# Four expert half-steps, six transposes and the chain for the row maxima are moved and rewritten in an early-fusion transformer kernel

## The chip, the cores and the metric

The kernel runs on one core of a Trainium2 chip. The metric is the device time of one execution in microseconds. The engines are TensorE (PE, with its weight loads as PEld), VectorE (DVE), ScalarE (ACT), GpSimd (POOL) and SyncE (SP), which issues most DMAs. Each runs its own program in order, and they wait for each other through semaphores.

## What is computed

Sixteen images and sixteen texts go through one block. A tokenizer makes 49 image tokens of each image; with a class token and 128 text tokens they are 178 tokens of 192 channels. An attention layer, a second attention layer with standardised logits, and a top-2 mixture of four experts follow. Cut to what the change touches:

```python
# second attention (inside the ffn)
logits = jnp.einsum('bqhd,bkhd->bhqk', Q, K) * scale
logits = gamma * _zscore_last(logits, T)
probs = jax.nn.softmax(logits, axis=-1)
...
x = _layernorm(src + attn, ln1_g, ln1_b)
gate_scores = jax.nn.softmax(x @ Wg.T + bg, axis=-1)
top2_val, top2_idx = jax.lax.top_k(gate_scores, 2)
combine = (jax.nn.one_hot(top2_idx, E, dtype=x.dtype) * top2_val[..., None]).sum(axis=-2)
h = jax.nn.relu(jnp.einsum('btd,edf->ebtf', x, W1) + b1[:, None, None, :])
y = jnp.einsum('ebtf,efd->ebtd', h, W2) + b2[:, None, None, :]
ff = jnp.einsum('ebtd,bte->btd', y, combine)
return _layernorm(x + ff, ln2_g, ln2_b)
```

The first attention (s = 0 in the kernel) masks the diagonal of its logits; the second (s = 1) does not.

## The kernel before

**Rounds.** The 16 images are taken as eight pairs. After a first part (tokenizer, first attention of pair 0, weight preparation) come nine rounds. Round p works on three pairs at once: the second attention of pair b = p, the first attention of pair a = p + 1, and the expert network of pair m = p - 1; it also starts the front (transposes, query, key, value) of pair nxt = p + 2. Rounds 2 to 5 are all alike. Round 0 has no experts yet; round 6 has no nxt; round 7 has neither a nor nxt; the last has only experts.

**What sets the order.** The order is written out by hand: `pe_round`, `act_round` and `dve_round` each list the parts of a round. The expert network is cut into 50 half-steps. Step (u, even) makes the hidden tile u of 24: five products (L674) into bank 4 or 5, followed by a ReLU on ScalarE (L709). Step (u, odd) is the second layer of tile u - 1: three products (L696) into banks 6 and 7. The last two are the turn of the combine weights with the last second layer, and the bias product (L684). VectorE adds an expert's result (L724) at the first odd step behind the expert's last tile, that is at steps 13, 25, 37, and at step 48. How many half-steps run at which named point of a round is a table: `FILL` for rounds 1 to 5 and the last, `FILL_A7` for round 6, `FILL_B7` for round 7. All three engines go through the same points with the same numbers. Round 0 and the first part fill with idle products instead (`WARM`, L770).

**A round on TensorE**, in order: half-steps ("start"), transposes of the normalised tokens (L787), "norm", query product (L795), "query", key product (L795), "key", value product (L803), transposes of the keys (L916, L917), "kc", product of keys with themselves (L927), "g", product with the queries (L933), "u", sum over a head (L939), "ss"; then the first maximum pass, "split", the turn of the maxima (L863), "rows", the exponential pass of a; then the second maximum pass of b (points `("max", 1)` behind each unit), "split", its L863, the output part of a, its exponential pass and output part; then the front of nxt, the rest of the half-steps, the transposes of x2 (L1006), the value product of nxt and the gate products (L1019).

**A maximum pass** has six units. A unit makes the logits of two heads in three banks (L830, L836; for s = 0 also the mask, L845); VectorE reduces each bank to its row maxima (L1368), and the next unit may overwrite a bank once it is read. Behind the pass VectorE splits the negated maxima into three bf16 parts (L1374 to L1380), TensorE turns them (L863), ScalarE copies them to `mrows` (L1097, L1098), and SyncE transfers them as three extra contraction rows, so that the exponential pass has them in its product.

**Waits the change touches.** The key product waits for ScalarE's query copies (`q_f32`) and for VectorE's centred tokens (`xc_ready`); the value product for ScalarE's key copies (`k_f32`); L927 for ScalarE's copy of the turned keys and for VectorE's value copies (`v_ready`, L1246, L1250). VectorE does in this stretch: centred tokens, `last.finish()` (norm and output of the pair before, L751 to L754), the split of the keys (L1236 to L1239), the value copies. A `Chain` is a row of operations on one engine of which each waits for the one before through a semaphore; `CHAIN_STEPS` holds how many links it counts.

## Time and profile before

| | us |
|---|---|
| median of 3 runs | 1234.02 |
| the runs | 1228.44, 1234.02, 1234.77 |
| the profiled execution | 1228.34 |
| its span | 1226.7 |
| TensorE busy | 1097.7 (89% of the span) |
| VectorE busy | 679.3 (55%) |
| ScalarE busy | 394.5 (32%) |
| mean granted TensorE clock | 0.947 |

A row of a timeline gives the start, the time from there to the end of the last of its instructions, the engine, the line, what is written from what, and how many; in brackets how long the engine was idle just before and whom it had waited for.
### The profile page before, as it was taken

The numbers are of one execution on the slowest core, as the hardware profiler recorded it, in microseconds if no ns is written. First come the engines' busy times: TensorE is split into PE (matmuls) and PEld (weight loads), VectorE is DVE, ScalarE is ACT, GpSimd is POOL, SyncE is SP. The second block draws the span as 40 slices with busy tenths as digits, with TensorE's granted clock in tenths as the row PEclk, the third lists the DMA queues.
The fourth block names the chain that finished last, engine by engine and source line by source line (L and its number), as shares of the span: only waits on it lengthen the run. The fifth ranks groups of instructions, "written<-read, shape, count | busy, mean of one in ns | idle before, by whom it ended". The sixth has DMA issues, their size and how long they took to land.

```text
span 1226.7 us, 19327 instructions
## 1 busy us (share of the span) xinstructions
PE 1097.7 (89%) x7731; PEld 809.0 (66%) x7731; DVE 679.3 (55%) x1890; ACT 394.5 (32%) x901; POOL 45.5 (4%) x81
## 2 busy tenths in 40 slices
PE   4898797888799999899989998999899989888895
PEld 3443464555486678568857875777588657676795
DVE  1378666564744666557654765476547643623432
ACT  1222132223324333443334333432343234223221
POOL 4200000100000000000000000000000000000000
PEclk8999899999989899989999998999899999788998
DMA  9100061422052014203320332042204220040000
GB/s 262 50 1 0 20 176 29 74 60 38 16 116 46 9 40 101 46 9 59 82 46 9 71 69 45 10 87 53 46 9 87 53 46 2 10 87 2 2 9 9
DMA packets 39441, 60.80 MB, mean 50 GB/s; under 512 B 6660, under 2 KB 31224, under 8 KB 38776
## 3 DMA queue, kind: packets, MB, share of 16 engines
q1 hardware_dynamic: 36256, 56.84, 21.5%
q10 hardware_dynamic: 3096, 2.74, 0.9%
q8 instruction: 61, 1.00, 0.4%
q14 instruction: 28, 0.23, 0.1%
HBM read 42.77 MB, written 16.34 MB: 48 GB/s over the span
## 4 chain that ended last, share of the span: by engine, by line
PE 63%; DVE 16%; ACT 4%; issue 2%; DMA 1%; SPq 1%; POOL 0%; DVEq 0%; POOLq 0%
PE PS L696 15%; PE PS L674 12%; DVE mx L1368 7%; PE PS L795 6%; PE PS L889 5%; PE PS L830 5%; PE PS L803 4%; PE PS L836 3%; PE PS L898 2%; PE PS L845 1%; DMA qst<-mrows 1%; PE PS L927 1%; PE PS L770 1%; PE PS L1019 1%; DVE acc L724 1%
## 5 line engine op out<-in xcount | busy, mean ns | idle before, releaser
L696 PE MATMUL PS<-w,hid 128*128 128x192 f32 x1152 | 231.1, 339 | 2.5 <-DVE acc L724 1.9
L709 ACT ACTIVATE hid<-PS,b 128x370 f32<-128x370 f32 x192 | 109.2, 569 | 316.7 <-PE PS L674 315.1
L696 PEld LDWEIGHTS PS<-w,hid 128*128 128x128 f32 x1152 | 197.8, 197 | 13.2 <-issue 5.1
L1368 DVE TENSOR_REDUCE mx<-PS 128x2 f32<-128x356 f32 x288 | 127.4, 519 | 131.7 <-PE PS L830 99.0
L1107 ACT ACTIVATE probs<-PS 128x356 f32<-128x356 f32 x288 | 110.9, 486 | 22.3 <-PE PS L830 12.8
L674 PE MATMUL PS<-x2T_hi,w_hi 128*128 128x370 f32 x192 | 91.9, 479 | 0.0
L845 PE MATMUL PS<-masks,ident_bf 128*128 128x256 bf16 (+1 forms) x288 | 73.4, 256 | 0.0
L889 PE MATMUL PS<-probs,va 128*17 128x178 f32 x1536 | 67.3, 315 | 6.4 <-ACT probs L1107 6.4
L795 PE MATMUL PS<-xT,w_at 96*96 96x370 f32 x192 | 68.2, 500 | 2.6 <-ACT xT L1067 1.7
L830 PE MATMUL PS<-kst,qst 96*128 96x178 bf16 x384 | 64.7, 264 | 6.3 <-issue 2.2
L770 PE MATMUL PS<-masks,ident_bf 128*128 128x356 bf16 x351 | 62.4, 327 | 4.0 <-POOL hid L1693 4.0
L674 PE MATMUL PS<-x2T_hi,w_lo 128*128 128x370 f32 x192 | 66.0, 344 | 0.0
L674 PE MATMUL PS<-x2T_lo,w_hi 128*128 128x370 f32 x192 | 65.8, 343 | 0.0
L674 PE MATMUL PS<-x2T_hi,w_rest 128*128 128x370 f32 x192 | 65.8, 342 | 0.0
L674 PE MATMUL PS<-x2T_lo,w_rest 128*128 128x370 f32 x192 | 65.6, 341 | 0.0
L830 PE MATMUL PS<-qst,kst 99*128 99x178 bf16 x384 | 54.6, 243 | 9.8 <-DMA qst<-mrows 6.1
L889 PEld LDWEIGHTS PS<-probs,va 128*17 128x17 f32 x1536 | 40.1, 97 | 22.4 <-ACT probs L1107 9.2
L1389 DVE RECIPROCAL rs<-PS 128x36 f32<-128x36 f32 x16 | 6.1, 382 | 86.9 <-PE PS L898 86.9
L770 PEld LDWEIGHTS PS<-masks,ident_bf 128*128 128x128 bf16 x351 | 34.7, 101 | 25.8 <-issue 6.3
L795 PEld LDWEIGHTS PS<-xT,w_at 96*96 96x96 f32 x192 | 31.2, 170 | 30.6 <-ACT xT L1067 5.3
L830 PEld LDWEIGHTS PS<-kst,qst 96*128 96x128 bf16 x384 | 24.9, 101 | 39.3 <-DVE mx L1368 29.1
L724 DVE SCALAR_TENSOR_TENSOR acc<-PS,comb,acc 128x192 f32<-128x192 f32 x72 | 25.6, 411 | 42.7 <-PE PS L696 42.5
(232 smaller groups left out, 1727.3 us busy)
## 6 DMA issues: line engine op xcount, KB each, us to landing
qst<-scr_q SPq DMA_DIRECT2D x96, 144.0 KB, 4.6
scr_q<-qs SPq DMA_DIRECT2D x16, 432.0 KB, 3.3
scr_k<-ks SPq DMA_DIRECT2D x16, 432.0 KB, 4.1
kst<-scr_k SPq DMA_DIRECT2D x16, 432.0 KB, 5.0
kst<-scr_k SPq DMA_DIRECT2D x16, 288.0 KB, 5.9
cols<-in_x_cols SPq DMA_DIRECT2D x6, 392.0 KB, 12.7
w<-in_w SPq DMA_DIRECT2D x1, 2304.0 KB, 29.4
kst<-scr_k SPq DMA_DIRECT2D x16, 144.0 KB, 6.3
```

Of the source, the lines that this page charges most:

```text
L674: ins = nc.tensor.matmul(PS[:, 4 + u % 2, 0:XN], w[:, f], x[:, plane, 0:XN], start=(k == 0), stop=(k == 4))
L696: ins = nc.tensor.matmul(tile_psum((6, 7), i), hid[u % 2][:, 128 * i:128 * i + 128], w2[:, u, :], start=(j == 0 and i != 1), stop=(j == FT ...
L709: nc.scalar.activation(hid[u % 2][:, 0:XN], PS[:, 4 + u % 2, 0:XN], ACT.Relu, bias=b1[:, u:u + 1]).then_inc(S["h_ready"], 1)
L724: ins = nc.vector.scalar_tensor_tensor(out=acc[:, i, :], in0=tile_psum((6, 7), i), scalar=comb[:, i, e:e + 1], in1=(acc if e else x2)[:, i ...
L770: nc.tensor.matmul(PS[:, 7, 0:T2], ident_bf[:], masks[:], start=True, stop=True)
L795: ins = nc.tensor.matmul(PS[0:HC, banks[m], 0:XN], w_at[:, w, k, HC * m:HC * m + HC], x[:, k, 0:XN], start=(k == 0), stop=(k == 1))
L803: ins = nc.tensor.matmul(tile_psum(banks, i), tile_cols(x, k, i), w_at[:, w, k, :], start=(k == 0), stop=(k == 1))
L830: ins = nc.tensor.matmul(PS[:, bank, T * b:T * b + T], still[0:rows_, h, TP * b:TP * b + NTXT], move[0:rows_, h, TP * b:TP * b + T], start ...
L845: ins = nc.tensor.matmul(own, ident_bf[:], m.rearrange("p (b j) -> p b j", b=2), start=False, stop=True, skip_group_check=True)
L889: ins = nc.tensor.matmul(PS[32 * q:32 * q + VW, 3, T * b:T * b + T], va[s][:, 2 * i + b, h, :], pr, start=(i == 0), stop=(i == 1), skip_gr ...
L1107: nc.scalar.activation(probs[:, u % PROB_UNITS, bank, :], PS[:, bank, 0:T2], ACT.Exp)\
L1368: nc.vector.tensor_reduce(out, PS[:, g, 0:T2].rearrange("p (b j) -> p b j", b=2), AX.X, ALU.max)\
```

## The change

Three things. The table moves four half-steps from "query" (4 to 2) and "key" (3 to 1) to the second maximum pass, one each behind its second to fifth unit. The transposes of x2 go ahead of the last half-step, the bias product. The split of the maxima takes six operations instead of nine, with three links instead of eight: the first part is cast straight from the maxima, the remainder is one operation from `mx`, and the third part is written as the difference itself.

```diff
-CHAIN_STEPS = {... "dve_max0": 8, "dve_max1": 8, ...
+CHAIN_STEPS = {... "dve_max0": 3, "dve_max1": 3, ...
 FILL = {
-    "start": 4, "norm": 1, "query": 4, "key": 3, "value": 0, "kc": 2, "g": 2, "u": 1, "ss": 2,
+    "start": 4, "norm": 1, "query": 2, "key": 1, "value": 0, "kc": 2, "g": 2, "u": 1, "ss": 2,
...
-    ("max", 1): (0, 0, 0, 0, 0, 0), ("split", 1): 2, ("turn", 0): 2, ("back", 0): 1, ("rows", 1): 1,
+    ("max", 1): (0, 1, 1, 1, 1, 0), ("split", 1): 2, ("turn", 0): 2, ("back", 0): 1, ("rows", 1): 1,
...
-            def rest(self):
-                self.steps(MOE_STEPS)
+            def rest(self, but=0):
+                self.steps(MOE_STEPS - but - self.done)
...
-            moe.rest()
+            moe.rest(1)
             if b is not None:
 
                 pe.wait_ge(S["x2_ready"], at(b, 1, 1))
...
                                                   x2_wide[:, i, 128 * h:128 * h + 128], ident[:])
                 ins.then_inc(S["x2T_psum"], 1)
+            moe.rest()
             if nxt is not None:
                 pe_value(pe, 0, nxt)
...
-            ch.link(nc.vector.tensor_scalar(mneg[:], mx[:], -1.0, None, ALU.mult))
-            for c in range(3):
-                ch.link(nc.vector.tensor_copy(mbf[:], mneg[:]))
-                ins = nc.vector.tensor_copy(mpart[:, :, c, :], mbf[:])
-                if c < 2:
-                    ch.link(ins)
-                    ch.link(nc.vector.tensor_tensor(mneg[:], mneg[:], mbf[:], ALU.subtract))
-            ins.then_inc(S["m_split", s], 1)
+            ch.link(nc.vector.tensor_scalar(mbf[:], mx[:], -1.0, None, ALU.mult))
+            nc.vector.tensor_copy(mpart[:, :, 0, :], mbf[:])
+            ch.link(nc.vector.scalar_tensor_tensor(out=mneg[:], in0=mx[:], scalar=-1.0, in1=mbf[:],
+                                                   op0=ALU.mult, op1=ALU.subtract))
+            ch.link(nc.vector.tensor_copy(mbf[:], mneg[:]))
+            nc.vector.tensor_copy(mpart[:, :, 1, :], mbf[:])
+            nc.vector.tensor_tensor(mpart[:, :, 2, :], mneg[:], mbf[:], ALU.subtract).then_inc(S["m_split", s], 1)
```

TensorE around the key product of the second attention (round 1), from the end of the "query" point to the value product, before. L795 is the key product, L696 and L674 are half-steps, L803 is the value product.

```order
L795 MATMUL PS<-oT,w_at 96x370 x4
L696 MATMUL PS<-w,hid 128x192 x3
L674 MATMUL PS<-x2T_hi,w_hi 128x370
L674 MATMUL PS<-x2T_hi,w_lo 128x370
L674 MATMUL PS<-x2T_lo,w_hi 128x370
L674 MATMUL PS<-x2T_hi,w_rest 128x370
L674 MATMUL PS<-x2T_lo,w_rest 128x370
L696 MATMUL PS<-w,hid 128x192 x3
L803 MATMUL PS<-w_at,xT 128x192 x6
```

The same place after:

```order
L674 MATMUL PS<-x2T_lo,w_rest 128x370
L795 MATMUL PS<-oT,w_at 96x370 x4
L696 MATMUL PS<-w,hid 128x192 x3
L803 MATMUL PS<-w_at,xT 128x192 x6
L916 MATMUL PS<-ident,k 128x96
```

One half-step is left between the two products where there were three; ahead of the key product two are left of four. All half-steps from here to the second maximum pass are thus four earlier ones in number, and VectorE's first L724 goes from the "kc" to the "ss" point.

TensorE in the second maximum pass, its last two units and the first half-step of the "split" point, before (L830 and L836 are a unit; the four units ahead stand like these):

```order
L830 MATMUL PS<-kst,qst 128x178 x4
L836 MATMUL PS<-kst,qst 64x178 x4
L830 MATMUL PS<-kst,qst 128x178 x4
L836 MATMUL PS<-kst,qst 64x178 x4
L696 MATMUL PS<-w,hid 128x192 x3
```

and after, from the second unit to the fourth:

```order
L830 MATMUL PS<-kst,qst 128x178 x4
L836 MATMUL PS<-kst,qst 64x178 x4
L696 MATMUL PS<-w,hid 128x192 x3
L830 MATMUL PS<-kst,qst 128x178 x4
L836 MATMUL PS<-kst,qst 64x178 x4
L674 MATMUL PS<-x2T_hi,w_hi 128x370
L674 MATMUL PS<-x2T_hi,w_lo 128x370
L674 MATMUL PS<-x2T_lo,w_hi 128x370
L674 MATMUL PS<-x2T_hi,w_rest 128x370
L674 MATMUL PS<-x2T_lo,w_rest 128x370
L830 MATMUL PS<-kst,qst 128x178 x4
L836 MATMUL PS<-kst,qst 64x178 x4
```

Units with a half-step between them, where the units followed each other.

VectorE behind a second maximum pass, before, with the semaphores that each operation waits for:

```order
L1374 TENSOR_SCALAR mneg<-mx 128x36 [waits s_used1]
L1376 CAST mbf<-mneg 128x36 [waits dve_max1]
L1377 CAST mpart<-mbf 128x3x12 [waits dve_max1]
L1380 TENSOR_TENSOR mneg<-mneg,mbf 128x36 [waits dve_max1]
L1376 CAST mbf<-mneg 128x36 [waits dve_max1]
L1377 CAST mpart<-mbf 128x3x12 [waits dve_max1]
L1380 TENSOR_TENSOR mneg<-mneg,mbf 128x36 [waits dve_max1]
L1376 CAST mbf<-mneg 128x36 [waits dve_max1]
L1377 CAST mpart<-mbf 128x3x12 [waits dve_max1]
```

and after:

```order
L1375 TENSOR_SCALAR mbf<-mx 128x36 [waits s_used1]
L1376 CAST mpart<-mbf 128x3x12 [waits dve_max1]
L1377 SCALAR_TENSOR_TENSOR mneg<-mx,mbf 128x36
L1379 CAST mbf<-mneg 128x36 [waits dve_max1]
L1380 CAST mpart<-mbf 128x3x12 [waits dve_max1]
L1381 TENSOR_TENSOR mpart<-mneg,mbf 128x3x12
```

Three operations are gone, and two of the six wait for nothing. The programs of SyncE and GpSimd are the same.

## Rows read from the trace of the kernel before

**Rows 1.** Page, part 1, TensorE: busy us (share of span) xinstructions.

```profile
PE 1097.7 (89%) x7731; PEld 809.0 (66%) x7731; DVE 679.3 (55%) x1890; ACT 394.5 (32%) x901; POOL 45.5 (4%) x81
```

**Rows 2.** Timeline of TensorE, 707 to 721 us: start, us, line, operation, count.

```profile
707.28 1.14 PE L696 MATMUL PS<-w,hid 128*128 128x192 f32 x6
...
710.95 2.65 PE L795 MATMUL PS<-oT,w_at 96*96 96x370 f32 x8
713.44 1.14 PE L696 MATMUL PS<-w,hid 128*128 128x192 f32 x6
...
716.25 2.12 PE L803 MATMUL PS<-w_at,xT 96*128 96x192 f32 x12
...
720.71 2.02 PE L927 MATMUL PS<-probs 128*96 128x96 f32 x16
```

**Rows 3.** Timelines of ScalarE and of VectorE, 707 to 720 us.

```profile
707.48 1.30 ACT L1077 ACTIVATE q<-PS,chan 96x256 f32<-96x256 f32 x4 [2.18 <-PE PS L795]
...
713.64 0.93 ACT L1091 COPY k<-PS 96x256 f32<-96x256 f32 x4 [1.92 <-PE PS L795]
...
714.60 0.53 DVE L1236 CAST ks<-k 96x712 bf16<-96x712 f32 x1 [0.69 <-ACT k L1091]
...
718.40 0.56 DVE L1246 TENSOR_TENSOR va<-PS,rows 128x384 f32<-128x384 f32 x1 [0.85 <-PE PS L803]
718.88 0.71 DVE L1250 TENSOR_TENSOR va<-PS,rows 50x192 f32<-50x192 f32 x2
```

**Rows 4.** TensorE, second maximum pass, round 3: timeline, then one row by windows.

```profile
637.22 0.48 PE L830 MATMUL PS<-kst,qst 96*128 96x178 bf16 x4
...
644.70 2.29 PE L696 MATMUL PS<-w,hid 128*128 128x192 f32 x6
...
647.87 0.49 PE L863 MATMUL PS<-ident,mpart 128*36 128x128 f32 x3
...
641.30:643.30 2.00, 2.00 (x14) 0.68 (x14) 2.00 (x6) 0.00 (x0) 0.00 (x0) 0.50 0.00 0
```

The last row is: stretch, its length, then busy us (count) of PE, PEld, DVE, ACT and POOL, the granted clock, the DMA share and GB/s.

**Rows 5.** Timeline, round 7's second maximum pass: TensorE, then one of VectorE.

```profile
1105.47 0.47 PE L830 MATMUL PS<-kst,qst 96*128 96x178 bf16 x4 [2.17 <-issue]
...
1107.62 0.44 PE L674 MATMUL PS<-x2T_hi,w_hi 128*128 128x370 f32 x1
...
1111.87 0.47 PE L830 MATMUL PS<-kst,qst 96*128 96x178 bf16 x4
...
1113.54 0.48 PE L830 MATMUL PS<-kst,qst 96*128 96x178 bf16 x4
...
1115.31 0.47 PE L830 MATMUL PS<-kst,qst 96*128 96x178 bf16 x4
...
1113.91 1.40 DVE L1368 TENSOR_REDUCE mx<-PS 128x2 f32<-128x356 f32 x3 [0.28 <-PE PS L830]
```

**Rows 6.** L863 in all (busy, mean ns, idle before), then timelines around the chain.

```profile
L863 PE MATMUL PS<-ident,mpart 128*36 128x128 f32 x48 | 7.8, 271 | 10.2 <-DVE mpart L1377 8.6 <-issue 1.6
...
207.02 0.49 PE L863 MATMUL PS<-ident,mpart 128*36 128x128 f32 x3 [0.64 <-DVE mpart L1377]
...
619.00 0.18 DVE L1374 TENSOR_SCALAR mneg<-mx 128x36 f32<-128x36 f32 x1
...
620.78 0.19 DVE L1377 CAST mpart<-mbf 128x36 f32<-128x36 bf16 x1
620.89 0.95 DVE L1354 SCALAR_TENSOR_TENSOR q<-q,chan,rem 96x712 f32<-96x712 f32 x1
```

**Rows 7.** Timelines of TensorE and VectorE around the bias product, round 3.

```profile
694.74 1.24 PE L684 MATMUL PS<-b,hid 4*128 4x192 f32 x6 [1.16 <-DVE acc L724]
695.91 0.88 PE L1006 MATMUL PS<-ident,x_wide 128*128 128x128 f32 x6
696.62 2.12 PE L803 MATMUL PS<-w_at,xT 96*128 96x192 f32 x12
...
697.72 0.96 DVE L1488 TENSOR_TENSOR x2T_lo<-PS,x2T_hi 128x768 fp32r<-128x768 f32 x1 [0.81 <-ACT x2T_hi L1190]
```

4 lines of the change are left out of this document (2 added, 2 removed).

## The prediction

> **What bounds the kernel now.** Read first the page's part 1: TensorE is busy for 89% of the span [rows 1], VectorE, the next, for little over half. So a microsecond counts only where TensorE stands still, runs at the half clock, or is made to. I then went along TensorE's timeline of one round (rounds p = 2 to 5 repeat every 119.5 us within 0.1; the rows are of p = 3 and the start of p = 4) and, wherever the change touches it, along the timelines of the engines it waits for. "Half-step" is one expert step: five products of L674 (one hidden tile) or three of L696 (its second layer). Four half-steps last from 707.28 to 710.95, 3.67 us, so a pair is 1.84 us [rows 2].
>
> **Part A: four half-steps leave the query and key points.** At the query point two stay (1.84 us). The key product then starts at 709.12 instead of 710.95. It needs ScalarE's query copies, which end at 707.48 + 1.30 = 708.78 [rows 3]: 0.34 us of margin, no new wait. It lasts 713.44 - 710.95 = 2.49 us [rows 2], to 711.61. At the key point one second-layer half-step stays, about 0.97, to 712.58. The value product overwrites the banks of the key and waits for ScalarE's key copies: those began 0.20 after the product and took 0.93 [rows 3], so they end at 712.74, and the product starts at about 712.85: a new wait of 0.27. From the value product to the product at L927 it is 720.71 - 716.25 = 4.46 us [rows 2], so TensorE is at L927 by 717.3. But L927 also waits for VectorE's value copies. VectorE finishes the pair before (moments, norm, output) at 714.60 - 0.69 = 713.91, and nothing here makes that earlier; the key split then takes 718.40 - 0.85 - 714.60 = 2.95, and the value copies 718.88 + 0.71 - 718.40 = 1.19 [rows 3]. That gives 718.1, and L927 starts at 718.17: a second new wait of 0.87. Against 720.71 this is 2.54 us won, of 3.67 moved away. In round p = 1 there is no pair to finish, the second wait is absent, and 3.41 is won. The first expert's accumulation on VectorE moves behind the product of L1348; it ends just before the first reduction of the first pass could start, so it costs nothing, with some 0.1 us to spare. **A: 4 x 2.54 + 3.41 = 13.6 us.**
>
> **Part D: the same four half-steps in the second maximum pass.** Today it takes 10.65 us from the pass's first product to L863 (637.22 to 647.87), and the second-layer half-step behind it lasts 2.29 us instead of 1.14, because the granted clock is 0.50, the 1.2 GHz level, from about 640.5 to 647.3; the row shown is in its middle [rows 4]. In front of the fall TensorE had been idling between the units of the pass, which follow VectorE's reductions. The last round already runs this pass with the very fill the change writes (0, 1, 1, 1, 1, 0), so its rows price it: two units take 1107.62 - 1105.47 = 2.15; a unit with a hidden-tile half-step 1113.54 - 1111.87 = 1.67; a unit with a second-layer one 1115.31 - 1113.54 = 1.77 [rows 5]. Order here: unit, unit, second, unit, hidden, unit, second, unit, hidden, unit. I take 2.1 + 1.08 for the first two and their half-step, then 1.67 + 1.77 + 1.67: the last unit starts at 8.3. VectorE starts 0.37 after it and needs 1.40 [rows 5], to 10.1; the shorter chain adds 1.1 (below), the hand-over 0.15: L863 at 11.3. TensorE itself is ready at 8.3 + 0.69 + 1.9 = 10.9 at full clock. So 10.65 becomes 11.3: **D: -0.65 us in each of five rounds, -3.3 us**, for 3.67 us of work absorbed. Behind L863 the order is the old one.
>
> **Part B: the chain for the maxima.** Nine operations run from 619.00 to 620.97. Linked ones follow each other at 0.22; an unlinked one lets the next start after 0.11 (620.78 to 620.89) [rows 6]. Six operations with three links come to 0.21 + 0.11 + 0.23 + 0.22 + 0.11 + 0.20 = 1.08 us against 1.97: 0.89 less. Is it on the path? TensorE idles 10.2 us in all in front of L863 [rows 6], in 11 places: the eight first-maximum passes, and the second pass of rounds 0, 6 and 7. Three of these waits are only 0.64 (the first is shown), the others 0.98 to 1.23. The copies, the row transfer and the exponential pass behind them start from L863, so the wait for the transfer moves with it and does not take the gain back. **B: 3 x 0.64 + 8 x 0.89 = 9.0 us.** The bounds for the unseen pitch of the new operations are 0.11 and 0.22 each.
> The Trainium skill (VectorE: DVE Perf Modes, "The DRAIN you can't avoid") says that leaving out the semaphores between operations saves nothing, since the next one waits for the pipe to drain. By that the chain would be 6 x 0.22 = 1.32 us, B 7.1 us. The row of L1354, which starts 80 ns before its predecessor ends, speaks against it here.
>
> **Part E: transposes ahead of the bias product.** TensorE waits 1.16 us for the fourth expert's accumulation before L684, then does the bias product, then six transposes from 695.91 to 696.62 [rows 7]. x2 has long been ready, so the transposes (0.71) go into the wait, of which 0.45 is left, and everything behind is 0.71 earlier. On VectorE the low part (L1488) today waits 0.81 for ScalarE's cast [rows 7]; the cast now starts 2.3 us earlier (1.16 of wait and 1.17 of bias product no longer stand before it), and what is late next is VectorE's own bias addition in front, which stays: the low part and the gate products come about 0.77 earlier. I take 0.75 in the rounds p = 1 to 7. **E: 5.3 us.** The last, lone block of expert steps has no transposes and gains nothing.
>
> **Sum.** 13.6 - 3.3 + 9.0 + 5.3 = 24.6 us. The profiled execution took 1228.3 us and gives 1203.7; against the median of 1234.0 the same sum gives 1209.4. The three runs lie 6 us apart and the page does not say why; I put the forecast between the two, at 1207.0, for the rounds' half-clock stretches, which may differ from run to run, are mostly gone.
>
> **Rivals.** (1) *The clock still falls in the filled pass.* For it: in the last round it did, with the same fill: hidden-tile half-step, unit and second-layer half-step took 1111.87 - 1107.62 = 4.25 us, where the full-clock rows give 2.76, and the pass 10.5 us, not 9.0 [rows 5]. Against: there TensorE had idled 2.17 us just before [rows 5], far more than in the steady rounds, and here only the first two units are unfilled. One slow stretch costs 1.5 us a round, 7.6 in all; two (as today) 3.4, 17 in all: 1215 to 1224.
> The Trainium skill (TensorE: Matmul & The Clock Gate, "A second HAM failure mode: psum-queue depth-cycling") says that short idles between groups of products, cycling through banks, are enough to make the clock swing. Today's pass agrees; the rule speaks against full clock wherever the waits between units stay.
> (2) *The four half-steps were covering waits in full.* If VectorE's finishing of the pair before slips (its output buffer, or its own start), L927 starts where it did, and A is nothing in the four rounds and in p = 1: 1207 + 13.6 = 1221. Against: its seven operations there run without a gap.
> (3) *Slower.* The thinner query and key points let the clock fall at the two new waits (0.27 and 0.87 us) as well as in the pass. Two slow stretches of 3.4 us at both places lose 6.8 us a round, 34 in all: 1241. It decides from a loss of 4.9 us a round, three such stretches. Against: the lone wait of 1.16 us in every round [rows 7] is longer than either and the products around it keep their full-clock length.
> (4) *The chain does not shorten beyond its three missing operations.* All six then follow each other at 0.22 [rows 6], 1.3 us: 2 us less gain, 1209, by itself inside the forecast's own range.
>
> **Numbers.** Forecast 0.64 (1200 to 1213; the low end is the profiled base with one half-clock stretch less, 1.7 us, in each of rounds 6 and 7), of which 0.2 is rival 4. Rival 1: 0.17. Rival 2: 0.11. Rival 3: 0.04. Other small losses that leave it within half a per cent (about what a measurement of this kernel tells from no change): 0.04. Range 1200 to 1223: it takes in rivals 1 and most of 2. Faster 0.92, same 0.05, slower 0.03.
>
> **What would show it.** In the changed profile: the round 116.0 us long instead of 119.5 in p = 2 to 5; from the second pass's first product to L863 11.3 us with the granted clock at 1.00 (D; 0.5 there is rival 1); a wait of 0.9 us of L927 on the value copies and of 0.3 us of the value product on the key copies (A; if L927's wait is over 3, rival 2); idle before L863 near 3 us in sum instead of 10.2, with about 0.4 in each steady second pass (B); 0.45 us before the bias product, and no wait of L1488 on the cast (E). Wrong would be new idle of TensorE in front of the first maximum pass or of the exponential passes.

## The result, and the profile after

The changed kernel took 1198.72 us in the median (1192.23 to 1201.45, four runs) against 1231.23 us for the kernel before (1228.42 to 1234.77, four runs): a ratio of 0.9727, 95% interval 0.9676 to 0.9778. The forecast was 1207.0 and the range 1200 to 1223, so the sign was right and the time lies 1.3 us below the range. The profiled execution took 1198.64 us with a span of 1197.0; the one before had 1226.7. That is 29.7 us less, where the sum had 24.6. A few executions of some kernels ran in a slower state, with a lower clock; the medians and ratios below leave them out.

The page's part 1, which answers to [rows 1]:

```profile
PE 1082.6 (90%) x7731; PEld 801.5 (67%) x7731; DVE 668.0 (56%) x1842; ACT 394.9 (33%) x901; POOL 43.7 (4%) x81
```

TensorE has the same 7731 instructions and is busy for 15.1 us less. The work did not shrink: fewer of its products ran at the 1.2 GHz level (mean granted clock 0.964, before 0.947). The other half of the gain is time in which TensorE had stood still. VectorE has 48 operations less, three in each of the sixteen chains.

**The points that lost half-steps** [rows 2, 3]. TensorE in round 3, key product, value product, L927:

```profile
582.73 2.65 PE L795 MATMUL PS<-oT,w_at 96*96 96x370 f32 x8
...
586.39 2.22 PE L803 MATMUL PS<-w_at,xT 96*128 96x192 f32 x12
...
591.64 2.07 PE L927 MATMUL PS<-probs 128*96 128x96 f32 x16 [0.51 <-DVE va L1251]
```

From key to value product it takes 3.66 us where it took 5.30, from value product to L927 5.25 where it took 4.46 (in the other steady rounds 5.24): the second is the new wait on VectorE's value copies that the prediction named.

**The filled second maximum pass** [rows 4]. TensorE in round 3, first unit, last unit and L863, and the same stretch as a row of the view by windows (stretch, length, busy us and count of PE, PEld, DVE, ACT, POOL, granted clock, DMA share, GB/s). Beside it the stretch of before, 637.22 to 647.87, whose clock was shown in its middle only:

```profile
626.85 0.48 PE L830 MATMUL PS<-kst,qst 96*128 96x178 bf16 x4
...
635.07 0.48 PE L830 MATMUL PS<-kst,qst 96*128 96x178 bf16 x4
...
638.03 0.49 PE L863 MATMUL PS<-ident,mpart 128*36 128x128 f32 x3 [0.17 <-issue]
```

```profile
626.85:638.03 11.18, 10.60 (x85) 7.87 (x82) 9.36 (x25) 1.79 (x5) 0.00 (x0) 1.00 0.01 1
```

```profile
637.22:647.87 10.65, 9.94 (x64) 5.59 (x61) 9.98 (x29) 0.52 (x2) 0.00 (x0) 0.68 0.01 2
```

Four half-steps more, 0.53 us longer, and the clock at its full level all through.

**The chain** [rows 6]. VectorE behind that pass, and what L863 waited for in all:

```profile
636.87 0.18 DVE L1375 TENSOR_SCALAR mbf<-mx 128x36 bf16<-128x36 f32 x1
637.09 0.19 DVE L1376 CAST mpart<-mbf 128x36 f32<-128x36 bf16 x1
637.20 0.19 DVE L1377 SCALAR_TENSOR_TENSOR mneg<-mx,mbf 128x36 f32<-128x36 f32 x1
637.42 0.18 DVE L1379 CAST mbf<-mneg 128x36 bf16<-128x36 f32 x1
637.63 0.19 DVE L1380 CAST mpart<-mbf 128x36 f32<-128x36 bf16 x1
637.74 0.19 DVE L1381 TENSOR_TENSOR mpart<-mneg,mbf 128x36 f32<-128x36 f32 x1
```

```profile
  issue: 0.8, 5
  DVE mpart L1381: 0.3, 1
```

0.22 us behind a linked operation, 0.11 behind an unlinked one; with the last 0.19 it is 1.06 us. TensorE's idle time in front of L863 falls from 10.2 us to 1.1.

**The transposes** [rows 7]. TensorE at the end of round 2's experts, then VectorE's low part, which no longer waits:

```profile
564.87 0.82 PE L1006 MATMUL PS<-ident,x_wide 128*128 128x128 f32 x6
566.20 1.24 PE L684 MATMUL PS<-b,hid 4*128 4x192 f32 x6 [0.51 <-DVE acc L724]
...
568.40 0.96 DVE L1488 TENSOR_TENSOR x2T_lo<-PS,x2T_hi 128x768 fp32r<-128x768 f32 x1
```

**Where the time went, round by round.** The second pass's L863 of each round is a landmark: 295.1 us in round 0 before and 292.6 after. Each cell holds the length between two landmarks and, behind the stroke, how much of it the trace's clock record has at the 1.2 GHz level, in us. The rows are the profiled executions, one each, of the kernels that are told of below (shift12, which is like after, is left out).

```
             0 to 1       1 to 2       2 to 3       3 to 4       4 to 5       5 to 6       6 to 7       7 to end
before       113.7/13.7   119.5/ 6.8   119.5/ 6.8   119.5/ 6.8   119.5/ 6.8   123.5/ 3.4   109.8/27.3   106.6/23.1
after        111.1/10.2   115.6/ 0     118.6/ 6.8   116.0/ 0     115.6/ 0     119.9/ 0     104.4/17.1   103.1/17.4
after_again  109.7/ 6.8   115.6/ 0     115.6/ 0     115.7/ 0     115.6/ 0     127.5/17.0   103.6/13.7   101.6/14.0
after_third  109.7/ 6.8   115.7/ 0     115.7/ 0     115.7/ 0     115.7/ 0     122.7/ 9.1   105.6/25.1   103.4/16.7
after_fourth 109.8/ 6.8   115.6/ 0     115.6/ 0     115.7/ 0     115.7/ 0     127.7/17.1   103.2/13.7   101.7/13.9
fill_only    112.7/10.2   119.9/ 3.4   119.6/ 3.4   119.5/ 3.4   119.9/ 3.4   125.6/12.9   107.2/21.3   104.8/20.1
end_fill     111.7/15.0   127.9/15.3   125.1/ 9.1   127.6/14.9   125.4/ 9.4   133.8/14.4   107.2/20.9   104.9/20.5
chain_only   112.8/13.7   119.4/ 6.8   119.0/ 6.5   120.2/10.6   119.2/ 6.8   122.2/ 2.8   105.9/21.1   103.5/17.6
turn_only    114.5/17.1   119.1/ 6.8   119.2/ 6.7   119.2/ 6.6   119.2/ 6.6   124.2/10.8   105.4/17.1   102.8/17.8
fill_turn    112.7/10.2   122.1/10.2   120.4/ 6.8   117.5/ 0     117.8/ 0     123.6/ 6.3   108.2/24.4   104.5/21.0
fill_chain   109.7/ 6.8   116.8/ 0     116.4/ 0     116.4/ 0     120.9/10.2   123.5/10.2   103.8/17.1   103.9/17.2
shift24      112.5/13.7   120.3/10.2   115.7/ 0     115.7/ 0     120.3/10.2   122.5/ 6.0   102.1/14.5   103.5/17.0
norm_late    109.7/ 6.8   114.9/ 0     115.0/ 0     117.9/ 6.8   115.6/ 0     120.3/ 3.4   108.2/20.5   103.1/17.3
last_fill    109.7/ 6.8   115.6/ 0     115.6/ 0     115.7/ 0     115.7/ 0     122.1/ 8.4   108.1/25.7   104.2/19.4
best1        109.8/ 6.8   114.9/ 0     114.9/ 0     117.9/ 6.8   114.9/ 0     126.6/19.6   106.9/17.9   102.8/17.8
last_warm    109.7/ 6.8   115.7/ 0     115.7/ 0     115.7/ 0     115.6/ 0     121.0/ 3.4   102.9/10.2   101.5/10.3
best2        109.8/ 6.8   115.0/ 0     115.0/ 0     117.9/ 6.8   115.0/ 0     121.1/ 6.8   105.5/13.7   101.6/ 9.9
best3        109.7/ 6.8   114.9/ 0     114.9/ 0     117.9/ 6.8   115.4/ 0     120.9/ 6.8   102.9/ 6.8   100.4/ 9.4
```

Three of the four steady rounds are 115.6 to 116.0 us long; the sum had 116.0. The one between landmarks 2 and 3 is 3.0 longer with the same work. Four rows by windows of the changed kernel (columns as above) show it by the clock:

```profile
403.77:519.41 115.64, 110.77 (x876) 85.96 (x876) 70.12 (x206) 44.56 (x106) 2.01 (x4) 1.00 0.26 52
519.41:638.03 118.62, 113.76 (x875) 89.26 (x876) 70.14 (x206) 44.63 (x106) 2.00 (x4) 0.97 0.25 50
...
989.48:1093.89 104.41, 91.49 (x610) 75.53 (x611) 50.58 (x150) 32.32 (x71) 1.83 (x2) 0.92 0.14 29
1093.89:1197.00 103.11, 84.84 (x585) 77.84 (x585) 32.54 (x111) 30.52 (x65) 0.67 (x1) 0.92 0.02 7
```

The last two answer to these of the kernel before:

```profile
1010.35:1120.16 109.81, 94.93 (x610) 78.32 (x611) 51.99 (x153) 32.31 (x70) 1.48 (x2) 0.88 0.13 28
1120.16:1226.70 106.54, 87.67 (x585) 80.46 (x585) 32.53 (x111) 30.18 (x64) 0.67 (x1) 0.89 0.02 6
```

What the loss in that one round looks like: TensorE behind the gate products. Two hidden-tile half-steps run at 0.31 us a product, and at 0.17 once the clock is back.

```profile
573.00 0.51 PE L674 MATMUL PS<-x2T_hi,w_lo 128*128 128x370 f32 x1
573.31 0.51 PE L674 MATMUL PS<-x2T_lo,w_hi 128*128 128x370 f32 x1
...
577.63 0.33 PE L674 MATMUL PS<-x2T_lo,w_hi 128*128 128x370 f32 x1
577.80 0.33 PE L674 MATMUL PS<-x2T_hi,w_rest 128*128 128x370 f32 x1
```

Summed by the table: up to the landmark of round 0 2.5 us are won (the sum had 1.9), from there to that of round 5 14.8 (17.8), behind it 12.5 (4.9). So in this profile the size was missed in the last rounds, and their time at the half clock fell from 53.8 us to 34.4. The three further profiles of the changed kernel divide the gain otherwise: 19.3 to 19.5 us between the landmarks of rounds 0 and 5, and 7.2 to 8.2 behind.

### The profile page after: what moved, and what is told of

The parts are those of the page before. It is cut to its first block, busy times and chain, and to the rows that moved or that the text cites. A ratio compares the mean times of both kernels' runs of the same rounds, so it can differ in the third digit from the quotient of the medians.

```text
span 1197.0 us, 19279 instructions
## 1 busy us (share of the span) xinstructions
PE 1082.6 (90%) x7731; PEld 801.5 (67%) x7731; DVE 668.0 (56%) x1842; ACT 394.9 (33%) x901; POOL 43.7 (4%) x81
## 4 chain that ended last, share of the span: by engine, by line
PE 65%; DVE 13%; ACT 4%; issue 2%; DMA 1%; SPq 1%; POOL 0%; DVEq 0%; POOLq 0%; ACTq 0%
PE PS L696 14%; PE PS L674 12%; PE PS L830 6%; PE PS L889 5%; PE PS L795 5%; PE PS L803 4%; PE PS L836 4%; PE PS L845 3%; DVE mx L1369 2%; PE PS L770 2%; PE PS L898 2%; PE PS L927 1%; DMA qst<-mrows 1%; PE PS L1020 1%; DVE acc L724 1%
## 5 line engine op out<-in xcount | busy, mean ns | idle before, releaser
L696 PE MATMUL PS<-w,hid 128*128 128x192 f32 x1152 | 225.6, 332 | 3.0 <-DVE acc L724 2.2
L696 PEld LDWEIGHTS PS<-w,hid 128*128 128x128 f32 x1152 | 191.4, 191 | 14.3 <-issue 2.5
L674 PE MATMUL PS<-x2T_hi,w_hi 128*128 128x370 f32 x192 | 89.7, 467 | 0.0
L795 PE MATMUL PS<-xT,w_at 96*96 96x370 f32 x192 | 67.9, 498 | 2.6 <-ACT xT L1068 1.7
L674 PE MATMUL PS<-x2T_lo,w_hi 128*128 128x370 f32 x192 | 65.5, 341 | 0.0
L674 PE MATMUL PS<-x2T_hi,w_rest 128*128 128x370 f32 x192 | 65.4, 341 | 0.0
L674 PE MATMUL PS<-x2T_hi,w_lo 128*128 128x370 f32 x192 | 65.2, 339 | 0.0
L674 PE MATMUL PS<-x2T_lo,w_rest 128*128 128x370 f32 x192 | 65.1, 339 | 0.0
L830 PE MATMUL PS<-qst,kst 99*128 99x178 bf16 x384 | 54.5, 243 | 9.9 <-DMA qst<-mrows 6.2
L830 PE MATMUL PS<-kst,qst 96*128 96x178 bf16 x384 | 56.9, 246 | 5.2 <-issue 1.8
L770 PEld LDWEIGHTS PS<-masks,ident_bf 128*128 128x128 bf16 x351 | 34.6, 101 | 25.7 <-issue 6.3
L795 PEld LDWEIGHTS PS<-xT,w_at 96*96 96x96 f32 x192 | 31.1, 170 | 30.7 <-ACT xT L1068 5.3
L724 DVE SCALAR_TENSOR_TENSOR acc<-PS,comb,acc 128x192 f32<-128x192 f32 x72 | 25.6, 411 | 42.9 <-PE PS L696 42.9
L830 PEld LDWEIGHTS PS<-qst,kst 99*128 99x128 bf16 x384 | 26.5, 97 | 34.2 <-issue 17.4
```

The source lines that it names most:

```text
L674: ins = nc.tensor.matmul(PS[:, 4 + u % 2, 0:XN], w[:, f], x[:, plane, 0:XN], start=(k == 0), stop=(k == 4))
L696: ins = nc.tensor.matmul(tile_psum((6, 7), i), hid[u % 2][:, 128 * i:128 * i + 128], w2[:, u, :], start=(j == 0 and i != 1), stop=(j == FT ...
L770: nc.tensor.matmul(PS[:, 7, 0:T2], ident_bf[:], masks[:], start=True, stop=True)
L795: ins = nc.tensor.matmul(PS[0:HC, banks[m], 0:XN], w_at[:, w, k, HC * m:HC * m + HC], x[:, k, 0:XN], start=(k == 0), stop=(k == 1))
L830: ins = nc.tensor.matmul(PS[:, bank, T * b:T * b + T], still[0:rows_, h, TP * b:TP * b + NTXT], move[0:rows_, h, TP * b:TP * b + T], start ...
```

## The experiments

The theory: the three parts work as costed, and the rest of the gain is TensorE's clock, which falls less often once its idle places are gone. The rival: the parts are worth more than costed by themselves. Of each kernel the table above has the profiled execution; ratios are to the kernel before. A single profile can be an odd one, so here is the mean time at the half clock over the executions that the medians are taken of (span, times one minus the mean granted clock, times two), with their number:

```
before      130 us (66)    fill_turn    97 (3)    norm_late    95 (4)    last_warm    69 (4)
fill_only   113 (8)        fill_chain   95 (4)    last_fill    93 (4)    best2        74 (6)
chain_only  134 (9)        changed      83 (18)   best1        99 (6)    best3        82 (6)
turn_only   119 (12)       end_fill    179 (5)
```

**fill_only: the table alone.**

```diff
-    "start": 4, "norm": 1, "query": 4, "key": 3, "value": 0, ...
+    "start": 4, "norm": 1, "query": 2, "key": 1, "value": 0, ...
-    ("max", 1): (0, 0, 0, 0, 0, 0), ...
+    ("max", 1): (0, 1, 1, 1, 1, 0), ...
```

> The kernel before with the table of the change alone: query 2, key 1, one half-step behind each of units 2 to 5 of the second maximum pass; old chain, old place of the transposes. Theory (the parts add up, and the clock keeps its full level in the filled pass): query and key stretch 2.67 us shorter a round, the pass with its hand-over 12.1 us instead of 10.65 since VectorE's long chain now stands open behind it, round 118.3 us instead of 119.5, and about 7 us off the whole (ratio near 0.994), with no half-clock stretch in the passes of rounds 1 to 5. Rival (nearly all of the gain is the clock, the moved work as such brings little): the round falls by 3 us or more with this part alone and the ratio is under 0.985.

Measured: 1231.08 us, 1.0014 (0.9975 to 1.0053): neither the 0.994 of the theory nor the rival. The stages did what they were to do (key to value product 3.66, value product to L927 5.24, the pass 12.08 at full clock), but the rounds stayed at 119.5 to 119.9. In rounds 2 to 5 the clock now falls at another place, from 578.4 us on in round 2, under 2 us behind the wait in front of the bias product (TensorE's timeline, then a row by windows, whose first 0.5 us are still at the full clock):

```profile
576.62 1.24 PE L684 MATMUL PS<-b,hid 4*128 4x192 f32 x6 [1.16 <-DVE acc L724]
577.79 1.01 PE L1006 MATMUL PS<-ident,x_wide 128*128 128x128 f32 x6
578.59 3.70 PE L803 MATMUL PS<-w_at,xT 96*128 96x192 f32 x12
```

```profile
577.90:581.30 3.40, 3.40 (x15) 3.40 (x16) 1.78 (x3) 0.80 (x1) 0.00 (x0) 0.57 1.06 144
```

The same at 697.9, 817.3 and 936.8 us. So the largest term of my sum, 13.6 - 3.3, is worth nothing alone: of the 2.7 us won at the points, 1.4 go into the longer pass (12.08 for 10.65, its chain still has nine operations), and 1.3 are lost here (5.37 us from the bias product to the gate products, not 4.08).

**end_fill: the four half-steps go to the end of the round, not into the pass.**

```diff
-    "start": 4, "norm": 1, "query": 4, "key": 3, "value": 0, ...
+    "start": 4, "norm": 1, "query": 2, "key": 1, "value": 0, ...
```

> The kernel before, with the four half-steps of query and key taken to the end of the round (the rest) instead of into the second maximum pass. Theory (taking them away saves 2.67 us there, but they cost 3.67 wherever TensorE is busy anyway): round about 120.5 us, the second pass as before, 10.65 us with the granted clock at 0.50, the whole 3 to 6 us longer than before (ratio 1.002 to 1.005). Rival (query and key were overfilled, and leaving them is the gain): faster than before by 1% or more.

Measured: 1275.48 us, 1.0386 (1.0331 to 1.044), four rounds of 125 to 128. The expectation missed a wait. All experts' steps slide four places later in the round, and with them VectorE's accumulation of the third expert, which so falls behind its norm of x2; the second layer that overwrites those banks waits 2.49 us for it:

```profile
577.29 1.21 PE L696 MATMUL PS<-w,hid 128*128 128x192 f32 x6 [2.49 <-DVE acc L724]
```

TensorE's waits of L696 on L724 are 14.4 us in all (1.9 before), and the half-clock time of the four steady rounds goes from 27 us to 49. So, in this kernel, where the half-steps went to mattered more than where they left from.

**chain_only: the six operations alone.**

```diff
-            ch.link(nc.vector.tensor_scalar(mneg[:], mx[:], -1.0, None, ALU.mult))
-            for c in range(3):
...
+            ch.link(nc.vector.tensor_scalar(mbf[:], mx[:], -1.0, None, ALU.mult))
+            nc.vector.tensor_copy(mpart[:, :, 0, :], mbf[:])
...
```

> The kernel before with the chain for the maxima alone (six operations, three links). Theory: 0.86 us at each of the eight first passes and at the second pass of rounds 0, 6 and 7, nothing at the second passes of rounds 1 to 5 (there TensorE reaches L863 later than the maxima do): 9.5 us, ratio 0.992, give or take one or two half-clock stretches of 1.7 us elsewhere. Rival (unlinked operations gain nothing, only three operations less): 0.66 us each, 7 us. Rival (the wait for the row transfer behind L863 takes it back): under 3 us.

Measured: 1225.04 us, 0.9966 (0.993 to 1.0002), less than the 0.992 of the theory. The first pass, to its L863, takes 9.64 us in place of 10.56. But the second pass goes from 10.65 to between 10.8 and 11.1: its half-clock stretch comes at 398.4, 517.8, 637.3, 756.8 and 876.2 us, 119.4 to 119.5 apart although the work in front is 0.9 shorter, and so covers more of the pass. A stretch of 3.4 us more, at 691.9, is in the round of 120.2 us.

**turn_only: the transposes alone.**

```diff
-            moe.rest()
+            moe.rest(1)
             if b is not None:
...
+            moe.rest()
```

> The kernel before with the transposes of x2 ahead of the bias product alone. Theory: 0.87 us in each of seven rounds, 6 us, ratio 0.995; the wait of L1488 on the cast gone, 0.5 us left before L684. If the 9 us that the last two blocks of the changed kernel were shorter than my sum are this part's doing, 10 us or more here; if they are the places where the clock falls, the last blocks of this run differ from before by multiples of about 1.7 us in either direction.

Measured: 1221.36 us, 0.9942 (0.9911 to 0.9973), the ratio that was expected. At its place the part gives 0.8 us (5.60 us from the last second-layer half-step to the gate products, not 6.39), and in the steady rounds 0.3 of it arrives: the second pass takes up to 11.1, with half-clock stretches 119.4 to 119.5 apart (398.0 to 875.9). By their ratios the single parts come to some 10 us together; all three at once give 29 to 34 in the four measurements of the changed kernel. Their time at the half clock tells the same: 17 and 11 us less and 4 more singly, 47 less together.

**fill_turn: the changed kernel with the chain of nine; fill_chain: the changed kernel with the transposes behind the bias product.**

```diff
# fill_turn, against the changed kernel
-            ch.link(nc.vector.tensor_scalar(mbf[:], mx[:], -1.0, None, ALU.mult))
...
+            ch.link(nc.vector.tensor_scalar(mneg[:], mx[:], -1.0, None, ALU.mult))
...
# fill_chain, against the changed kernel
-            moe.rest(1)
+            moe.rest()
```

> The changed kernel with the old chain (nine operations, eight links): the moved half-steps and the transposes, not the chain. In fill_only the rounds 2 to 5 kept a period of 119.5 us although the parts gave 118.3, because the clock fell in every round right behind the wait of 1.16 us for the bias product. Theory (that wait and the gate products behind it are the next place where the clock falls, and the transposes take it away): rounds 2 to 5 at 117.4 us, half-clock time of the whole under 100 us, ratio 0.980 to 0.985, more than fill_only and turn_only together (1.0014 and 0.9942). Rival (the parts are independent, the clock's falls are chance): ratio 0.995.

> The kernel before with the moved half-steps and the short chain, the transposes in their old place. Theory: by the parts the round is 116.5 us; the wait of 1.16 us before the bias product is still there and the clock falls behind it in most rounds, so the rounds are 117 to 118 us and the ratio 0.985 to 0.990, with the half-clock stretches of the rounds at the gate products. Rival (the chain, not the transposes, ends the falls): rounds of 116.5 us without half-clock stretches, ratio 0.977.

Measured: fill_turn 1219.01 (three executions), 0.9869 (0.9789 to 0.9949); fill_chain 1208.23, 0.9802 (0.9741 to 0.9862). The rounds without a half-clock stretch add up: 115.6 with all parts, 116.4 to 116.8 without the transposes (they are worth 0.8 to 1.2, costed at 0.75), 117.5 to 117.8 without the short chain (worth 1.8 to 2.2, costed at 2 x 0.89 = 1.78). So the rival falls: at full clock each part is worth about what was costed. What differs is how many rounds of the profile keep the clock: none with one part, two of four in fill_turn, three in fill_chain and in the changed kernel's first profile. Both expectations missed a step. They took the bias wait for the place that makes the falls; but fill_chain has it too (1.16 us in every round), and behind only two of its first five the clock falls (798.6 and 918.1 us), so that wait alone doesn't make a fall; its ratio lies nearer to that of the rival (the chain ends the falls). fill_turn, without the wait, has two rounds with a fall. The fourth pairing, chain and transposes without the moved half-steps, was not run.

**shift12 and shift24: more idle products in front of round 0, nothing else.**

```diff
-            pe_warm(14)
+            pe_warm(38)    # shift24; 26 in shift12
```

> The changed kernel with 12 more idle products (L770) ahead of round 0, which push everything behind by about 0.9 us and change nothing else. Theory (where the clock falls in the last rounds depends on when they are reached): the half-clock stretches behind 1000 us are other ones, and the rest of the program is longer or shorter by steps of about 1.7 us. Rival (the last rounds are shorter because of their own content): same stretches, shifted by 0.9 us, the whole 0.9 us longer.

> As shift12 with 24 more idle products, about 2.8 us. Theory: another set of half-clock stretches again, time within 1192 to 1206 us. Rival: the changed kernel's stretches, 2.8 us later, and 1201.5 us.

Measured: 1198.45 and 1210.98 us, one execution each. The twelve pushed nothing: they went into a wait that TensorE has there in any case (row of the changed kernel), so that this run is no test of a shift.

```profile
235.75 0.86 PE L787 MATMUL PS<-ident,xn 128*96 128x128 f32 x6 [1.02 <-DVE xn L1230]
```

Its landmarks lie within 0.2 us of those of the changed kernel, and from the first of them on, within 0.3 us, the half-clock stretches too. With twenty-four, round 0 ends 4.3 us later and the kernel 12.4 us later: two steady rounds have 10.2 us of half clock each and last 120.3, the other two 115.6 and 115.7. Two rows by windows of it:

```profile
409.40:529.70 120.30, 115.40 (x876) 90.83 (x877) 70.16 (x206) 44.70 (x106) 2.01 (x4) 0.96 0.25 50
529.70:645.30 115.60, 110.75 (x875) 85.93 (x876) 70.07 (x206) 44.54 (x106) 2.01 (x4) 1.00 0.26 52
```

The same 875 to 877 products, the same waits, 4.7 us apart. One execution doesn't show that the shift did it, since repeats of the changed kernel (below) differ as well; it does show how much the place of the falls can move.

**after_again, after_third and after_fourth: the changed kernel three times more.**

> The changed kernel as it is, once more, for its spread and for the places of its half-clock stretches. In the first profile they were at 568, 1032, 1080 and 1131 us; with twelve idle products more at the start they were at the same places, and with twenty-four more at others, and the run was 12 us longer, although the work behind was the same. If the places hang on the timing of the start alone, they are at 568, 1032, 1080 and 1131 again within a microsecond, and the time is 1198 to 1199; if they hang on something that differs from run to run, other runs lie 5 to 10 us away, with their mean clock moving along (half as many microseconds as are spent at the lower clock).

> The changed kernel a third time, as the partner of the two runs above on the same chip. The time so far was 1191.5 to 1204.9 us in eight executions, their low-clock time 71 to 99 us. Expected: a median of 1198 to 1200 and the same spread; a steady round of 115.6 us where no half-clock stretch falls into it, 3.0 more with one of 6.8 us, 4.6 more with one of 10.2 us.

> The changed kernel as the partner on the same chip: 1196 to 1199 us in the median, single executions from 1191 to 1205, and no interval of its ratio that lies above or below that of the earlier repeats.

Measured: 1199.44 (1191.52 to 1204.94), 1196.23 (1192.21 to 1202.01) and 1197.23 (1195.79 to 1199.25); ratios 0.9764, 0.972 and 0.9766. The stretches are not at the places of the first profile, so these don't hang on the program alone: no fall in any steady round of the three, more between landmarks 5 and 7. All eighteen executions of the changed kernel lie between 1191.5 and 1204.9, median 1197.9, fourteen of them under 1200; their mean time at the low level is 83 us. The 66 of the kernel before that were timed beside the experiments lie between 1221.0 and 1242.6, median 1228.6, mean 130 us at the low level. Among the executions of one kernel the time rises by 0.4 (after) to 0.6 us (before) for each microsecond more at the low level, which accounts for over four fifths of the variance.

The clock records hold something that none of these runs was made to test. In each profile all starts and ends of half-clock stretches lie on one even raster of times, which stands differently against the program in each execution. Eight profiles have the same program up to landmark 5. In five of them (after_again, after_third, after_fourth, last_fill, last_warm) the landmark of round 0 lies within 0.15 us of a time of the raster, and no steady round has a fall. In after and shift12 it lies 0.5 and 0.6 us behind one, and both have the one fall at 568 us. In shift24 it lies 1.1 us ahead of one, and there are two falls. So what differs between executions goes with where the program stands against the raster; that this is the cause was not tested.

**norm_late: on VectorE the last three operations of the pair before go behind the product of L1348.**

```diff
             def finish(self, part=0):
...
+                if part == 1:
+                    self.ch = ch
+                    return
+                self.tail(ch)
...
-            last.finish()
+            last.finish(1)
...
                                     q32[1][:, :, :, 0:T], ALU.mult).then_inc(S["prod_ready"], 1)
             moe.point("u")
+            last.tail()
```

> The changed kernel with one move: on VectorE the last three operations of the finishing of the pair before go behind the product of L1348, so that the value copies of this pair come some 2.3 us earlier. It tests the step of the prediction that put the wait of 0.9 us at L927 on the value copies. By it L927's wait (0.8 to 0.9 us in rounds 2 to 7) goes or shrinks below 0.2, from the value product to L927 5.24 us become 4.4, and the round 115.6 becomes 114.8: some 4 us, about 1195 if the half-clock stretches stay. A rival: L933 and L939, which wait for VectorE's work behind it, wait longer by as much (the three operations now stand there), and the round stays 115.6. The stretches can move the time by 5 us either way, so the stage lengths decide, not the time.

Measured: 1203.04 us, 0.9792 (0.9756 to 0.9828), not faster than the changed kernel (1199.44, 0.9764 on the same chip). The stage did what it was to do. L927 (here L938) follows the half-step in front without a wait, and from the value product it takes 4.57 to 4.58 us, not 5.24:

```profile
586.24 1.14 PE L696 MATMUL PS<-w,hid 128*128 128x192 f32 x6
587.22 2.02 PE L938 MATMUL PS<-probs 128*96 128x96 f32 x16
```

The round is 114.9 to 115.0 in the two rounds ahead of a fall (115.6 in the one behind it). But the round from landmark 3 to 4 has a fall of 6.8 us and takes 117.9: 3.0 us, which is what 0.7 us in each of four rounds had won. All four kernels with this move (best1, best2, best3 below) have it in their profiles at 682 to 685 us. So here too the edit is worth about what was computed, and in the profile the clock takes it back.

**last_fill: five of the last round's half-steps go into its idle places. best1: this and norm_late together.**

```diff
-    "start": 0, "norm": 0, "query": 3, "key": 2, "value": 0, "kc": 0, "g": 0, "u": 0, "ss": 17,
+    "start": 1, "norm": 1, "query": 3, "key": 2, "value": 0, "kc": 1, "g": 1, "u": 1, "ss": 12,
```

> The changed kernel with five of the seventeen half-steps that stand behind the score sums in the last round spread over its idle places (start, norm, key copies, value wait, first product): only the last round's table row differs. It tests what the half-clock stretches of the last rounds are worth. TensorE idles there 0.5, 0.9, 0.9, 0.7 and 1.0 us at these places, 4 us, of which the half-steps (0.85 to 1.1 each) cover some 3.5: by that sum alone about 1195. If the stretches at 1032 and 1080 (10.2 and 6.8 us) follow from those idle places, they go too, which is worth up to 8.5 us: 1187. If they follow from VectorE's waits elsewhere, the clock stays and the time is 1195. A rival: VectorE's expert work, moved earlier with them, delays the copies that TensorE waits for, and nothing is won.

> Both moves together: the finishing's last three operations behind the product of L1348, and the last round's five half-steps spread over its idle places. Sum of the two: 8 us below the changed kernel, about 1190, ratio to the kernel before 0.967; with the half-clock stretches as now. If the two meet in the last round (the half-step at the value wait then has nothing to cover) 0.9 us less is won. If the gains are handed back by more half-clock stretches, as with the single parts of the change, it is 1195 to 1199.

Measured: last_fill 1203.53, 0.9804 (0.9771 to 0.9837); best1 1204.13, 0.9807 (0.978 to 0.9834). Both miss: 4 to 5 us above the changed kernel on the same chip, with no fewer falls (25.7 and 17.9 us of half clock between landmarks 6 and 7). Moving half-steps also moves ScalarE's and VectorE's part in them; whether that or the places of the falls cost the time was not separated.

**last_warm: idle products in three waits of the last rounds. best2: this and norm_late together. best3: best2 with fewer idle products.** They keep TensorE busy without moving anything else.

```diff
+            if b is not None and nxt is None:
+                pe_idle(22)
             if b is not None:

                 pe.wait_ge(S["w_split"], 1)
                 pe.wait_ge(S["x2T_lo"], at(b, 1, 1))
...
                 pe_turn_in(pe, 1, b)
+                if m is not None and a is None:
+                    pe_idle(8)
# best3
-                    pe_idle(8)
+                    pe_idle(6)
...
-                pe_idle(22)
+                pe_idle(13)
```

> The changed kernel with idle products (they write a bank that nobody reads) in places where TensorE waits in any case: 22 of them in front of the gate products at the end of the last two rounds (a wait of 2.07 us each), 8 behind the norm transposes of the last round (a wait of 0.88 us). No expert work moves and VectorE does what it did. It tests whether the clock falls at 1032 and 1131 us because TensorE idles there. If it does, the stretches that begin there (10.2 and 6.8 us in the first profile of the changed kernel) go or move, the low-clock time behind the second pass of round 6 falls from 30 to 36 us to 20 to 26, and the stretch from there to the end gets 3 to 6 us shorter than 204 to 207 us. A rival: these falls follow from the twelve gate products themselves, which have few columns and stay; then the stretches stay too and the time is 1198 to 1200. Another: the idle products delay the work behind them, up to 2 us longer.

> The idle products of the run before, together with the finishing's last three operations behind the product of L1348, whose steady rounds measured 114.9 us where TensorE's clock stayed up, 0.7 less than the changed kernel. If the idle products keep the clock up in the last rounds, this is 3 to 8 us below the changed kernel, about 1193; if they don't, it is as the move of the three operations alone, 1198 to 1204.

> The kernel best2 with fewer idle products: 13 instead of 22 in front of the gate products, 6 instead of 8 behind the norm transposes. In last_warm the 22 took 3.2 us (0.145 each) in a wait of 2.07, so they put the gate products of the last two rounds off by 1.07 us each; 13 take 1.9 and should fit. Expected: from L684 to the first gate product 3.3 us again, the last two intervals 2 us shorter than in best2 at the same half-clock time, 1190 us, some 6 us below the changed kernel on the same chip. A rival: with the wait only just filled the clock falls there as before (half-clock stretches at 1030 and 1130 us), and the time is that of best2 or above, 1192 to 1198.

TensorE in front of the gate products, in after_again and in last_warm, where L775 is the idle products and L1029 the first gate product; behind the latter two rows by windows, the last two intervals of the table:

```profile
1034.33 1.24 PE L684 MATMUL PS<-b,hid 4*128 4x192 f32 x6 [0.51 <-DVE acc L724]
1037.63 0.24 PE L1020 MATMUL PS<-gate_a,x2T_hi 128*128 128x8 f32 x1 [2.07 <-DVE x2T_lo L1488]
```

```profile
1027.54 1.24 PE L684 MATMUL PS<-b,hid 4*128 4x192 f32 x6 [0.51 <-DVE acc L724]
1028.71 3.49 PE L775 MATMUL PS<-masks,ident_bf 128*128 128x356 bf16 x22
1031.91 0.29 PE L1029 MATMUL PS<-gate_a,x2T_hi 128*128 128x8 f32 x1
```

```profile
987.38:1090.26 102.88, 92.18 (x641) 76.65 (x642) 50.49 (x150) 32.41 (x71) 1.33 (x2) 0.95 0.14 30
1090.26:1191.80 101.54, 85.32 (x607) 77.11 (x607) 32.56 (x111) 30.44 (x65) 0.67 (x1) 0.95 0.02 7
```

Measured: last_warm 1195.39 (1190.66 to 1199.72), ratio 0.9715 (0.9665 to 0.9764), and no fall in or right behind either gate wait: they start at 1033 and 1132, 1038 and 1137, 1030 and 1133, 1035 and 1134 us in the four profiles of the changed kernel. From landmark 6 to the end its half-clock time is 20.5 us against 34.4, 27.7, 41.8 and 27.6. The stretch itself is 204.4 us long, against 207.5, 205.2, 209.0 and 204.9: the gain is less than the falls were worth, since the gate products come 1.07 us later, twice. A fall of 10.2 us stands at 1051.7, among the three waits of round 7 that were left (after_third has one at 1054.3). In time nothing was won that can be told: the changed kernel on the same chip had 1196.23 and 0.972. best2: 1192.2 (1189.79 to 1204.06), 0.97 (0.9658 to 0.9741), about as expected. best3 puts nothing off: the gate product starts 3.31 us behind L684, as in the changed kernel, and in its profile no fall stands there; from landmark 6 to the end it takes 203.3 us with 16.2 at the half clock:

```profile
1028.33 1.24 PE L684 MATMUL PS<-b,hid 4*128 4x192 f32 x6 [0.51 <-DVE acc L724]
...
1031.64 0.24 PE L1040 MATMUL PS<-gate_a,x2T_hi 128*128 128x8 f32 x1
```

Yet its median is 1195.11 (1192.89 to 1203.7), 0.9766 (0.9735 to 0.9797), not the 1190 expected, where the changed kernel on that chip had 1197.23 and the same ratio; and its mean time at the half clock over six executions is 82 us, that of the changed kernel. So in one profile thirteen products kept the clock up at these two places, and whatever they save is too little to be told from the spread of the rest: both kernels beat the one before for certain, but the changed one only by 2 to 4 us in the median, within overlapping intervals.

## Why the prediction was right, and where it was wrong

**Part A** held. Query to key product and key to value product took what was computed (4.40 and 3.66 us), and the wait of L927 on the value copies appeared, though its row lists 0.51 us of the 0.87 computed (norm_late, which removes it, gains 0.67). In steady rounds 2.7 us were won, 2.54 costed. No round lost it to a slipping finish, which was rival 2; norm_late then showed that this very wait, and no other, stood there.

**Part D** held: 11.18 us against 11.3, at clock 1.00, the last unit 8.22 behind the first (costed 8.3). Rival 1, that the clock still falls in the filled pass, did not come in the steady rounds. What the prediction left out is where else it would fall. It read the clock's fall as a property of the pass. fill_only shows that it was one of several places: with the pass filled, the fall came behind the bias wait in each of rounds 2 to 5.

**Part B** held in sum (L863's idle time fell by 9.1 us, costed 9.0), with one step wrong: the three places with 0.64 us of idle time were capped at 0.64, and gave 0.8 (round 0, second pass: 10.40 us before, 9.59 after). The ends of products are modelled, so an idle time that a row shows is no cap to the last tenth. The Trainium skill (VectorE: DVE Perf Modes, "The DRAIN you can't avoid") says that leaving out semaphores between operations saves nothing, by which the prediction estimated the chain at 1.32 us; the same section also says that a next operation that is not held starts earlier. The rows of the chain above, with 0.11 behind each unlinked operation, agree with the latter and decide for 1.06. Rival 4 fell with it.

**Part E** held: the wait in front of the bias product is 0.51 (costed 0.45), L1488 waits no longer, and the stage is 0.8 shorter (costed 0.75), which turn_only shows there; as whole rounds the gain shows in fill_chain alone.

**The size** is what failed, in two steps: the base, and the term for what the clock gives back. First, **the base**. The sum gave 1203.7 against the profiled execution and 1209.4 against the median of three runs, and I went between them. The 66 executions of the kernel before that were timed later have a median of 1228.6: the profiled one, 1228.3, was typical, and the three runs lay high. That is 3.3 us of the miss of 8.3.

Second, **what the clock gives back**. The sum counted it in the filled passes of rounds 1 to 5 alone, five stretches of 6.8 us or 34 us at the half clock, and put it at nothing elsewhere; the low end allowed one stretch of 1.7 us less in each of rounds 6 and 7. Measured are 43 us less at the half clock in the profiles (128.9 and 85.6) and 47 in the means (130 and 83). At the 0.4 to 0.6 us for each that the executions show, the 9 to 13 us that were not counted are worth 4 to 8 us (an estimate); 5 us are missing against the profiled execution, 6 between the medians of 1228.6 and 1197.9. In the profile that the result came with, the excess lies behind the landmark of round 5: 19.4 us of half clock fewer, and 12.5 us shorter where 4.9 were summed, against 3.0 us lost between landmarks 0 and 5, mostly in one steady round and in round 1. In the three further profiles it is 7.2 to 8.2 us behind that landmark, and 19.3 to 19.5 where 17.8 were summed ahead of it; there the steady rounds are 115.6 to 115.7 us long and not 116.0. Which idle place made which of the vanished falls stays open. That idle places make falls was shown for the gate waits alone, by last_warm, and those the change did not shorten (2.04 us before, 2.07 after). The range was too narrow on this side: the eighteen executions of the changed kernel alone spread over 13 us, and its low end lay inside their spread. Fourteen of them lie below it, so that the miss by 1.3 us is no accident of the four runs. The gate wait of round 7 before:

```profile
1161.12 0.34 PE L1019 MATMUL PS<-gate_a,x2T_hi 128*128 128x8 f32 x1 [2.04 <-DVE x2T_lo L1488]
```

**Rival 3** (the clock falls at both new waits) came nowhere in the changed kernel; end_fill is akin to it: the move of half-steps makes waits there, falls come with them, and the kernel is 3.9% slower.

What was shown: about what each part is worth at full clock; that filling the two waits in front of the gate products takes away the falls there (in all fifteen profiles of this case with both waits open, a half-clock stretch covers the first gate product or begins at most 1.4 us behind it, both times; in the three with them filled, neither time); that the time between executions goes with the time at the low level. What is not shown: why a fall comes in one steady round and not in the next of the same kernel (the raster above fits, untested), and which part of the change took away which fall. The distance of 119.4 to 119.5 us between the falls in chain_only and turn_only needs no force that holds the round at its old length: on a raster distances change in whole steps only, and in turn_only, whose steady rounds are 119.1 to 119.2 us long, the stretches slide through the pass by 0.3 us a round.

## What to carry to other kernels

Cost a part of a change twice: what it saves at full clock, and what half-clock time stands behind the idle places that it closes; the first adds up, the second doesn't: here single parts took away 17 us of it at most, all three 47. Idle products in a wait that nothing else can fill kept the clock up there in the profiles, but they cost what they overshoot, and no gain in time clear of the spread was measured; try them, and count over several executions. And compare the mean granted clock of the executions before the times: here one and the same kernel spread over 13 us, mostly with its time at the half clock, so that a few microseconds between two medians say little about an edit.
